# Attention of a macaron block: parts of q and k stacked along the contraction by on-chip DMA, probabilities weighed in 32 bits

## The reference

```
q, k, v = (inputs @ w_q.T), (inputs @ w_k.T), (inputs @ w_v.T)     # (b, t, 16 heads, 16)
scores  = einsum('bqhd,bkhd->bhqk', q, k);  causal mask to -inf
attn    = softmax(scores / sqrt(256));  ctx = einsum('bhqk,bkhd->bqhd', attn, v)
return ctx @ w_o.T + b_o
x = x + 0.5 * ffn(layernorm(x)); x = x + attn(layernorm(x)); x = x + 0.5 * ffn(layernorm(x))
```

## Time and profile before

| | |
|---|---|
| median of 3 runs | 439.52 us (436.39 to 440.93) |
| the profiled execution | 440.74 us, of which 438.6 us span from first to last instruction |
| busy: PE, DVE, ACT, POOL | 408.5, 300.8, 257.1, 247.7 us |
| granted TensorE clock over the span | 0.973 of full |

### The profile page before, as it was taken

One profiled execution on the slowest core, in us unless ns is written; L12 is line 12 of the kernel. 1 busy time (PEld: TensorE's weight loads), 2 busy tenths in 40 slices (PEclk: granted clock), 3 DMA queues, 4 the chain that ended last, 5 costly groups with the idle time before them and its releaser, 6 DMA issues.

```text
span 438.6 us, 10176 instructions
## 1 busy us (share of the span) xinstructions
PE 408.5 (93%) x2911; PEld 333.9 (76%) x2912; DVE 300.8 (69%) x613; ACT 257.1 (59%) x638; POOL 247.7 (56%) x307
## 2 busy tenths in 40 slices
PE   7768999999999889799999999888799999999996
PEld 4536888888888867588887888764488888888884
DVE  6767996865556697777677676966365575556566
ACT  2706885555655455788787787822155655655552
POOL 5136445866467349657777577210365586754850
PEclk9679999999999999989999999996999999999999
DMA  8929931111211630000000000007551212112136
GB/s 278 371 68 347 389 100 59 47 51 60 59 48 36 190 109 1 1 1 2 4 1 0 0 0 0 1 1 252 153 184 49 62 37 72 60 48 52 44 103 208
DMA packets 25738, 38.90 MB, mean 89 GB/s; under 512 B 3056, under 2 KB 20720, under 8 KB 25712
## 3 DMA queue, kind: packets, MB, share of 16 engines
q1 hardware_dynamic: 19088, 24.41, 16.3%
q0 software_dynamic: 4544, 12.07, 9.4%
q10 hardware_dynamic: 2080, 2.10, 1.4%
HBM read 29.37 MB, written 9.19 MB: 88 GB/s over the span
## 4 chain that ended last, share of the span: by engine, by line
PE 65%; DVE 12%; DMA 10%; issue 5%; ACT 3%; POOL 2%; SPq 1%; DVEq 0%; ACTq 0%; POOLq 0%
PE bank L1301 24%; PE bank L1323 12%; PE bank L1459 7%; PE bank L1470 4%; PE bank L1311 3%; DMA xn_scratch<-arena 3%; PE bank L1224 3%; DMA w_out<-y_scratch 3%; PE bank L1426 2%; PE bank L1277 2%; PE bank L1506 2%; DMA arena<-xn_scratch,gather_row 2%; DVE w_lo L876 1%; DMA y_scratch<-arena,scatter_row 1%; PE bank L1460 1%
## 5 line engine op out<-in xcount | busy, mean ns | idle before, releaser
L509 POOL DMA_INDIRECT arena<-xn_scratch,gather_row x46 | 50.8, 1105 | 72.7 <-PE bank L1277 42.1
L515 POOL DMA_INDIRECT y_scratch<-arena,scatter_row x42 | 60.2, 1434 | 34.3 <-ACT arena L681 31.2
L1301 PE MATMUL bank<-w_hi,xT_hi 128*128 x184 | 62.6, 421 | 1.2 <-ACT xT_hi L640 1.2
L990 DVE TENSOR_TENSOR wo_lo<-w_out,wo_hi 128x1024 fp32r<-128x1024 f32 x46 | 60.8, 1321 | 4.1 <-PE bank L1323 1.9
L995 DVE TENSOR_TENSOR gT_lo<-bank,gT_hi 128x512 fp32r<-128x512 f32 x46 | 31.7, 689 | 39.3 <-ACT gT_hi L655 39.2
L1301 PE MATMUL bank<-w_hi,xT_lo 128*128 x184 | 58.1, 397 | 0.0
L1301 PE MATMUL bank<-w_lo,xT_hi 128*128 x184 | 57.8, 395 | 0.0
L593 POOL TENSOR_TENSOR k_head<-k_hi,head_mask 128x256 fp32r<-128x256 f32 x64 | 38.7, 625 | 29.1 <-PE bank L1460 22.2
L648 ACT ACTIVATE arena<-bank 128x512 f32<-128x512 f32 x46 | 27.5, 598 | 45.7 <-PE bank L1301 45.7
L670 ACT ACTIVATE wo_hi<-w_out 128x1024 fp32r x46 | 48.8, 1060 | 6.0 <-issue 4.1
L979 DVE TENSOR_TENSOR xT_lo<-bank,xT_hi 128x256 fp32r<-128x256 f32 x46 | 19.5, 424 | 39.0 <-ACT xT_hi L640 38.9
(11 more groups left out here) (180 smaller groups left out, 968.8 us busy)
## 6 DMA issues: line engine op xcount, KB each, us to landing
w_raw<-in_win_t SPq DMA_DIRECT2D x8, 1024.0 KB, 9.7
w_out<-in_wout_t SPq DMA_DIRECT2D x16, 512.0 KB, 8.0
w_out<-y_scratch SPq DMA_DIRECT2D x16, 256.0 KB, 4.9
xn_scratch<-arena ACTq DMA_DIRECT2D x2, 1024.0 KB, 8.7
x<-in_x SPq DMA_DIRECT2D x4, 256.0 KB, 3.6
out<-x SPq DMA_DIRECT2D x4, 256.0 KB, 2.1
arena<-xn_scratch,gather_row POOLq DMA_INDIRECT x46, 3.5
y_scratch<-arena,scatter_row POOLq DMA_INDIRECT x46, 3.0
```

The source lines that it names most:

```text
L509: pool.indirect_dma_start(out=xb[j % 2][:, :], out_offset=None, in_=xn_dram, in_offset=bass.IndirectOffsetOnAxis(ap=gather_row[:, j:j + 1] ...
L515: pool.indirect_dma_start(out=y_dram, in_=y[j % 2][:, :], in_offset=None, out_offset=bass.IndirectOffsetOnAxis(ap=scatter_row[:, j:j + 1], ...
L990: dve.tensor_tensor(wo_lo[:, :, :], w_out[:, bass.ds(e, 1), :, :].rearrange("p o c d -> p (o c) d"), wo_hi[u][:, :, :].bitcast(F32), ALU.s ...
L1301: last = pe.matmul(bank[2 * half + u][:, :], tok[u][:, k, :], wts[:, bass.ds(e, 1), k, half * H:(half + 1) * H], start=(part == 0 and k == ...
```

## The change

- The weights of q and k are laid out so that a chunk's channels come in two groups of 4 heads, channel by channel. `stack` on SP's queue then copies, for each chunk and group, three parts of q (high, high, low) and of k (high, low, high) from 64 partitions into 16 partitions each, below each other: 12 DMAs of 64 KB a chunk, 96 in all. A head's three products are now one contraction over 48 partitions. `mask_keys` and `k_head` go.
- `scores` issues two tail matmuls of 256 columns and two head matmuls of 128 columns a pair (one a head), on 48 partitions that begin at 0 or 64, for tail of pair n and head of pair n-1 together, then the two mask matmuls. Head scores have two banks.
- The turned probabilities are copied once in f32: one half of a pair by DVE, the other by ACT. v is one f32 tile. `weigh` is 6 f32 matmuls a pair. `divide` moves to DVE and reads the bank directly; `add_up` goes.
- The steps are written out (35 of them), with chunks 5 steps ahead of use, and the last experts' scores are ordered around the last `project_out`.

```diff
+            def stack(kk):
+                c = kk % DK
+                q_stack, k_stack = stacks[c]
+                sp.wait_ge(k_hi_ready, kk + 1)
+                sp.wait_ge(qk_ready, kk + 1)
+                for g in range(2):
+                    if kk >= DK:
+                        sp.wait_ge(head_scored, (kk - DK) * CPAIRS + CPAIRS - 1 + g)
+                    rows = slice(GROUP * g, GROUP * (g + 1))
+                    for n in range(STACK):
+                        at = slice(GROUP * g + HD * n, GROUP * g + HD * (n + 1))
+                        for to, part in ((q_stack, (q_hi, q_hi, q_lo)[n][c]), (k_stack, (k_hi, k_lo, k_hi)[n][:, c, :])):
...
+                            sp.dma_start(to[at, :, :].bitcast(F32), part[rows, :].bitcast(F32)).then_inc(stacked[c][g], 16)
...
-            def mask_keys(b, s):
...
+            def scores(tail, head):
+                jobs = []
+                if tail is not None:
+                    kk, g = tail // CPAIRS, tail % 2
+                    pe.wait_ge(stacked[kk % DK][g], 16 * 2 * STACK * (kk // DK + 1))
...
+                    reach(pe, tail_probs_ready, 2 * (tail - 2) + 2)
...
+                    reach(pe, head_probs_ready, 2 * (head - 2) + 2)
...
+                for g, to, tile, width, _ in jobs:
+                    q_stack, k_stack = stacks[g // CPAIRS % DK]
+                    rows = slice(g % 2 * GROUP, g % 2 * GROUP + STACK * HD)
+                    for hh in range(2):
+                        s = g % CPAIRS // 2 * 2 + hh
+                        pe.matmul(to[:, hh * SEQ:hh * SEQ + width], q_stack[rows, s, tile * P:(tile + 1) * P],
+                                  k_stack[rows, s, 0:width], start=(hh == 0), stop=False, skip_group_check=True)
+                for g, to, tile, _, scored in jobs:
+                    pe.matmul(to[:, :].rearrange("p (h k) -> p h k", h=2)[:, :, tile * P:(tile + 1) * P], ident_b[:, :],
+                              bc(neg_mask[:, :], 1, [P, 2, P]), start=False, stop=True, skip_group_check=True)\
+                        .then_inc(scored, 1)
...
+            def weigh(g):
...
+                    pe.wait_ge(pT_ready[hh], g + 1)
+                    for i, (qt, kt) in enumerate(((0, 0), (1, 0), (1, 1))):
+                        last = pe.matmul(bank[5][:, qt * D + h * HD:qt * D + (h + 1) * HD], pT[g % 2 * 2 + hh][:, i, :],
+                                         v[:, 2 * b + kt, h, :], start=(kt == 0), stop=(kt == qt), skip_group_check=True)
...
+            def attend():
+                chunk(0)
+                values(0, 2)
+                turn(1, (1,))
+                chunk(1)
+                turn(1, (2,))
+                pe.wait_ge(x_added, TILES - 2)
+                values(2, 4)
+                pe.wait_ge(x_added, TILES)
+                for n in range(QPAIRS + WEIGH_LAG):
+                    scores(n if n < QPAIRS else None, n - 1 if 1 <= n <= QPAIRS else None)
+                    if n == 0:
+                        turn(1, (3,))
+                        values(4, 6)
+                    elif n == 1:
+                        values(6, 8)
+                    if 0 <= n - TURN_LAG < QPAIRS:
+                        turn_probs(n - TURN_LAG)
+                    if n >= WEIGH_LAG:
+                        weigh(n - WEIGH_LAG)
+                    if (n + CHUNK_AHEAD) % CPAIRS == 0 and DK <= (n + CHUNK_AHEAD) // CPAIRS < CHUNKS:
+                        chunk((n + CHUNK_AHEAD) // CPAIRS)
+                    if n > DIVIDE_LAG and (n - DIVIDE_LAG - 1) % HPAIRS == 0:
+                        turn_context((n - DIVIDE_LAG - 1) // HPAIRS)
+                    if n > DIVIDE_LAG + 1 and (n - DIVIDE_LAG - 2) % HPAIRS == 0:
+                        project_out((n - DIVIDE_LAG - 2) // HPAIRS)
+                    if n >= QPAIRS + 1:
+                        turn(2, (n - QPAIRS - 1,))
...
+                turn_context(BATCH - 1)
+                score_experts(1, range(TPAIRS - 2))
+                project_out(BATCH - 1)
+                score_experts(1, (TPAIRS - 2,))
+                warm(WARM_SCORES)
```

More of the change, by code:

```diff
@@ L352, in reach, with head @@
                 eng.wait_ge(signal, count)
[L354 to L368, removed]
+        def head(p, hh):
+            return p // CPAIRS * HPC + p % 2 * GROUP_HEADS + p % CPAIRS // 2 * 2 + hh
         def bc(ap, axis, shape):
@@ L579, in _ @@
                     add_bias(1, bo, i - 1, 1)
-            def mask_keys(b, s):
[L583 to L606, removed]
+            add_bias(1, bo, TPAIRS - 2, 2)
             inverse_root(2, 0, TPAIRS - 1)
@@ L750, in _, with chunk @@
             act.wait_ge(x_added, TILES)
[L752 to L755 removed]
+            def chunk(kk):
+                c = kk % DK
+                act.wait_ge(qk_done, kk + 1)
+                if kk >= DK:
+                    for g in range(2):
+                        act.wait_ge(stacked[c][g], 16 * 2 * STACK * (kk // DK))
                 act.activation(k_hi[:, c, :], bank[7][:, SEQ:2 * SEQ], ACT.Copy).then_inc(k_hi_ready, 1)
@@ L758, in chunk, with values @@
                                scale=1.0 / SEQ ** 0.5).then_inc(qk_hi_ready, 1)
[L760 to L774, removed]
+            def values(first, last):
+                for t in range(first, last):
+                    act.wait_ge(v_done, t + 1)
+                    act.activation(v[:, t, :, :], bank[VBANK[t % 4]][:, 0:D].rearrange("p (h d) -> p h d", h=HEADS), ACT.Copy)\
+                        .then_inc(v_ready, 1)
@@ L1212, in _, with attend @@
-            sweep(dve, step)
+            def attend():
+                chunk(0)
+                chunk(1)
+                for n in range(QPAIRS + WEIGH_LAG):
+                    if n >= DIVIDE_LAG and (n - DIVIDE_LAG) % HPAIRS == 0:
+                        divide((n - DIVIDE_LAG) // HPAIRS)
+                    if 1 <= n <= QPAIRS:
+                        max_head(n - 1)
+                    if n < QPAIRS:
+                        max_tail(n)
+                    if n > DIVIDE_LAG + 2 and (n - DIVIDE_LAG - 3) % HPAIRS == 0:
+                        add_attention((n - DIVIDE_LAG - 3) // HPAIRS)
+                    if 0 <= n - TURN_LAG < QPAIRS:
+                        copy_turned(n - TURN_LAG)
+                    if n > DIVIDE_LAG + 3 and (n - DIVIDE_LAG - 4) % HPAIRS == 0:
+                        measure_batch((n - DIVIDE_LAG - 4) // HPAIRS)
+                    if (n + CHUNK_AHEAD) % CPAIRS == 0 and DK <= (n + CHUNK_AHEAD) // CPAIRS < CHUNKS:
+                        chunk((n + CHUNK_AHEAD) // CPAIRS)
+                    if n == QPAIRS:
+                        sum_up(0, BATCH - 1)
+                    if n > QPAIRS:
+                        scale(2, n - QPAIRS - 1)
+                scale(2, TPAIRS - 2)
+                divide(BATCH - 1)
+                add_attention(BATCH - 1)
```

416 lines of the change are left out of this document (157 added, 259 removed).

## The result

| | before | after |
|---|---|---|
| median, us | 439.72 (4 runs) | 453.52 (450.1 to 458.58, 4 runs) |
| ratio, 95% interval | | 1.03 [1.0177, 1.0424] |
| profiled execution, us | 440.74 | 458.58 |
| its span, us | 438.6 | 456.8 |
| its mean granted TensorE clock | 0.973 | 0.915 |

The change makes the kernel 3% slower; the forecast was 436. The profiled execution of the changed kernel is the slowest of its four, and it has the lowest clock of them (0.915; the others 0.923 to 0.935).

The account below looks back on a forecast made before the run. PE's instructions, one behind the other, bound attention; its step grows from 2.49 to 2.81 us. Gains 1.2 + 1.7 - 1.0 + 1.4 = 3.3 take 440.74 to 437.4 profiled, 436 as median; range 426 to 446.

Parts of the forecast that it names:

- All stay under 2.81, so PE sets the pace: Attention steps: ACT at most 2.3, DVE 1.6, so PE's 2.81 us sets the step and most of 6.7 us waits go.
- D: Start of attention: stacking DMAs late, second group 7.6 us later, PE idles and its clock may fall; 444 us, chance 0.15.
- The step at full clock: PE's attention step: scores, masks, turned pieces, weighing and one run-out of 0.14 sum to 2.81 us, 0.32 more than now.
- The weighing: PE's step: 12 f32 instructions at 0.108 each take 1.30 us against 0.46, a loss of 0.84.
- The scores: PE's step: two tail matmuls 0.23 us, a gain of 0.56, and two head matmuls 0.24, a gain of 0.11.
- since time goes by columns: Tail scores: holding data on only 48 of 128 partitions gives no gain; 256 columns take 0.117 us each.
- Rival B: Attention step: tail and head scores run side by side and switches cost nothing; step 2.43 to 2.5, 427 us, chance 0.22.
- A: Attention step as summed from PE's instructions: 2.65 to 2.95 us, total 432 to 440 us, likeliest 436, chance 0.45.
- C: Attention step: both switches empty the pipeline (0.34 each), narrow head matmuls run at 0.216; step 3.20, 447 us, chance 0.18.
- The other engines: Attention step: ACT at most 2.3 us, DVE 1.6, POOL loses four maskings a pair; all under 2.81.
- The stacking DMAs: SP's queue: issues 0.50 us each, landing 2.1; hidden in steady state, first chunk exposed, step 0 at 171.2 instead of 167.65.
- The end: From pair 31's turn to the last division: 10.1 us against 11.8; after it 1.0 lost and 1.4 gained.

Follow-up runs that it names:

- experiment 1: The changed kernel with one more f16 matmul of 512 columns in each step, ahead of the turned pieces: 441.83 us, ratio 1.0048.
- Experiment 8: The changed kernel with one more f16 matmul of 256 columns and 128 rows in each step: 438.57 us, ratio 1.0014.
- (5): The kernel before with the 32-bit weighing alone, p and v in float32 without low parts, scores as they were: 450.57 us, ratio 1.0281.

## Why the prediction was wrong

- **The step that failed** is "All stay under 2.81, so PE sets the pace", taken with a step summed from rows that all stand at a granted clock of 1.00. That TensorE sets the pace was right: over 185 to 300 us the view of waits lists none of its matmuls, and its busy time is 114.92 of 115.00 us, at a mean clock of 0.82. That its pace is what the rows of before say was an assumption that I did not write down and gave no bound. I let the clock fall only in D, and there because PE would idle. It fell while PE was busy throughout. Half clock over some 48 us is 24 us; experiment 1 gave 12 of them back in spite of 7 us of useless work, and 8 gave 15 back with 3.5. Pair 8 had its turn at 204.28 where 196.3 was forecast, and pair 31 at 292.74 instead of 276.1, though at full clock a step was shorter than forecast.
- **The step at full clock** was predicted 2.81 and is 2.66. Masks 0.24 (measured 0.23) and turned pieces 0.66 (0.65) are right. The weighing, 1.30, is 1.26 where a chunk follows it (182.43 to 183.69) and 1.34 where the scores follow: the 0.08 more is the change from 128 rows to 48, for which 0.14 was taken. The scores, 0.47, are 0.44 in sum, but not for the reason given: "since time goes by columns" failed, for a matmul of 48 rows takes 0.2 over 256 columns, near the 0.216 that was taken as the upper bound, and two of them run side by side. The two errors cancel, which is luck.
- **Rival B** had the mechanism, head and tail scores side by side, and with it one of the signs named for A being wrong ("starts of head and tail scores nearly together"). Its size, 2.43 to 2.5, is too low because each of the matmuls is slower. 2.66 lies at the low end of A's 2.65 to 2.95. B and C both counted on the geometry of the matmuls for their time alone; it acted on the clock as well.
- **The weighing** "eats more than both gains in the scores": right. Alone (5) it costs 12 us.
- **The other engines** were priced right, and ScalarE and VectorE wait for TensorE.
- **The stacking DMAs**: issues 0.64 apart and not 0.50, landing 2.6 and not 2.1. Steps 0 to 4 began at 172.31, 176.18, 179.15, 181.11 and 185.59, against 171.2, 174.2, 176.7, 178.9 and 183.4: 1.1 to 2.5 us late. For steps 0 and 1 that is this term: the sixth and the twelfth issue, at 169.63 and 173.45, with 2.6 to landing, give 172.2 and 176.05. Behind them the clock of 0.74 and 0.83 up to 180 has a part. Hidden afterwards, as said. D did not come.
- **The end**: 10.1 forecast, 303.69 + 0.69 - 292.74 = 11.6 measured, partly at half clock. From the end of the division to the leaving of the last normed rows it was 289.07 to 296.04, 7.0, and is 304.38 to 314.56, 10.2: 3.2 lost where 1.0 was forecast, again partly at half clock (0.62 over 304 to 308). Those rows are turned (314.58) as they leave (314.56), and from their leaving to the first gather (326.54; before, 309.20) it is 12.0 us instead of 13.2, so 1.2 of the 1.4 us forecast behind the earlier trace rows are gained.
- **The sum at a full clock**: span times clock is 418; the forecast span of 438.6 - 3.3 = 435.3 at before's 0.973 would be 424. By this, the clock is more than the whole miss: at before's clock the changed kernel would have come 6 us under the forecast. Experiment 8, the changed kernel with its clock held and 3.5 us of filler in it, is at 438.6, inside the range.

The Trainium skill, TensorE: Matmul & The Clock Gate, Part 1, has the clock set by how busy the PE has been and lists half rate as "Idle/cold". This case's trace does not agree: 0.50 in windows in which PE is busy 4.00 of 4.00 us.

## What to carry to other kernels

A busy TensorE is not a fast one: look at the granted clock of each stage, and when a change takes columns or rows away from TensorE, give the forecast a case in which the clock falls although the engine never waits. If it has fallen, try one dense matmul per step before anything else; here 0.11 us of it per step was worth 15 us. Price a matmul that fills half of the rows by a row of its own kind, not by its columns, and look at the starts, not the durations, to see what runs side by side and what a change of height costs. Halving the columns of a matmul gains nothing while it runs beside one that keeps them. Parts that are ready early should be sent before those that are not.

## What the runs showed of the hardware

- TensorE's granted clock was 0.50 (1.2 of 2.4 GHz) for up to 13.6 us at a stretch (238.7 to 252.3) while it ran back to back scores of 48 rows, transposes and 16-column float32 matmuls, and went back by itself in between (after the projections of a chunk, 200.59 to 204.28, it was 0.92 from 204 to 208 and then 1.00).
- The same f16 matmul of 256 columns, once per step, held the clock with 128 rows (438.57 us) and did not with 48 (473.29); whether by its height or by the changes of height that it adds is open.
- Two 32-bit matmuls of 48 rows, one in partitions from 0 and one from 64, ran side by side: 0.41 us for two tail matmuls alone, 0.36 for two head matmuls alone, 0.44 for all four. Over 256 columns one of 48 rows took 0.2 us, one of 128 rows 0.117.
- Going from matmuls of 128 rows to 48 cost 0.08 us ahead of the scores (last weighing matmul to first score 0.19 against 0.11 between two weighing matmuls), and there and back around the filler of 48 rows 0.25.
- An issue of a 64 KB copy within SBUF takes SyncE 0.59 us, one every 0.64, and it lands after 2.6.
